# Adding the experts' rows into the token sums by the scatter itself (layer 1's MoE)

## What is computed

```
gate_logits = xf @ Wg + bg                      # xf = layernorm(t)
top_w, top_i = top_k(gate_logits, 2)
top_w = softmax(top_w)
w_dense = sum(one_hot(top_i, E) * top_w)
for e in range(E):
    h = gelu(xf @ W1[e] + b1[e])
    out = out + w_dense[:, e] * (h @ W2[e] + b2[e])
t = t + out                                     # then turned back to (channels, places)
```

## Time and profile before

| | us |
|---|---|
| median of 3 runs | 2480.7 (2469.35 to 2482.45) |
| the profiled execution, its own time | 2486.87 |
| its span in the trace | 2485.1 |

### The profile page before, as it was taken

How to read it: one execution, slowest core, us unless ns; L and a number is a source line. 1 busy time by engine, 2 the same in 40 slices (tenths; PEclk the granted TensorE clock), 3 DMA queues, 4 the chain that set the end, 5 groups by cost and what they waited for, 6 DMA issues and landing times. The chain is left out here.

```text
span 2485.1 us, 83832 instructions
## 1 busy us (share of the span) xinstructions
PE 2015.4 (81%) x28694; PEld 1524.5 (61%) x28695; DVE 2062.4 (83%) x3713; ACT 1732.2 (70%) x2708; POOL 790.9 (32%) x604
## 2 busy tenths in 40 slices
PE   6749999999999999999996208856896229999994
PEld 3327666666666766666664206643684129999992
DVE  5779999999999999999997646759797457777775
ACT  5569999999999999999984415537686335555551
POOL 3432124241431331231440553430364532222220
PEclk9869999999999999999997559985997559999996
DMA  2013323232323232323232233442112341111116
GB/s 81 1 34 89 84 77 89 72 92 70 92 71 91 71 90 71 90 72 89 73 85 84 87 131 104 116 126 95 45 68 84 112 135 51 48 47 47 51 44 209
DMA packets 285209, 202.98 MB, mean 82 GB/s; under 512 B 153395, under 2 KB 259846, under 8 KB 284870
## 3 DMA queue, kind: packets, MB, share of 16 engines
q1 hardware_dynamic: 271168, 163.57, 22.8%
q0 software_dynamic: 12960, 35.73, 3.9%
q10 hardware_dynamic: 998, 2.62, 0.3%
HBM read 68.98 MB, written 108.60 MB: 71 GB/s over the span
## 5 line engine op out<-in xcount | busy, mean ns | idle before, releaser
L595 DVE TENSOR_TENSOR plow<-prob 128x1024 f16<-128x1024 f32 (+1 forms) x1024 | 1127.1, 1171 | 3.7 <-ACT prob L506 3.7
L506 ACT ACTIVATE prob<-scores 128x1024 f32<-128x1024 f32 x1024 | 999.5, 1025 | 88.9 <-PE scores L638 58.5
L658 PEld LDWEIGHTS outp<-vs,prob 128*128 128x128 bf16 x7680 | 515.3, 98 | 279.8 <-issue 219.9
L658 PE MATMUL outp<-vs,prob 128*128 (+1 forms) x7680 | 603.6, 193 | 25.0 <-DVE plow L595 12.4
L638 PE MATMUL scores<-qT,kT 128*128 (+1 forms) x2048 | 610.6, 380 | 7.5 <-DMA kT<-shift_rows 2.7
L660 PE MATMUL outp<-vs,plow 128*128 (+1 forms) x7680 | 601.2, 193 | 0.0
L660 PEld LDWEIGHTS outp<-vs,plow 128*128 128x128 f16 x7680 | 502.8, 97 | 57.9
L448 POOL TENSOR_TENSOR osum<-osb 128x128 f32<-128x128 f32 x64 | 269.9, 4217 | 783.4 <-DVE rec L600 783.4
L1476 POOL DMA_INDIRECT expert_rows<-m1eyo,m1edest x71 | 108.0, 1521 | 304.5 <-DVE m1eyo L1448 275.5
L1347 PE MATMUL m1eph<-m1exT,m1ew1c 128*128 128x128 f16 x3408 | 203.4, 220 | 0.3 <-ACT m1exT L1384 0.3
L1347 PEld LDWEIGHTS m1eph<-m1exT,m1ew1c 128*128 128x128 f16 x3408 | 194.5, 98 | 1.0 <-ACT m1exT L1384 0.5
(11 more groups left out here) (393 smaller groups left out, 3335.4 us busy)
## 6 DMA issues: line engine op xcount, KB each, us to landing
sorted_rows<-zero SPq DMA_DIRECT2D x128, 522.0 KB, 4.7
staged<-qk SPq DMA_DIRECT2D x73, 128.0 KB, 2.3
m0exr<-sorted_rows SPq DMA_DIRECT2D x71, 130.5 KB
m1exr<-sorted_rows SPq DMA_DIRECT2D x71, 130.5 KB, 2.0
ls_got<-expert_rows SPq DMA_DIRECT2D x8, 1024.0 KB, 6.0
na_staged<-in_L_ffn_W_dram SPq DMA_DIRECT2D x16, 512.0 KB, 3.6
m1dstg<-in_L_ffn_W_dram SPq DMA_DIRECT2D x16, 512.0 KB
m1cgot<-expert_rows SPq DMA_DIRECT2D x8, 1024.0 KB
```

The costliest lines, as they stand in the source:

```text
L506: act.activation(prob[g % PBUF][:, :], scores[g % 2][:, :], ACT.Exp, scale=1.0 / (QK_SCALE * QK_SCALE)).then_inc(prob_ready, 1)
L595: dve.tensor_tensor(l[:, 0:n], p[:, 0:n], high(p)[:, 0:n], ALU.subtract).then_inc(low_ready, 1)
L658: pe.matmul(to, high(prob[g % PBUF])[:, cols], v, start=(g == 0 and i == 0 and j == 0), stop=False, skip_group_check=True)
```

## The change

`sums_dram` is a new tensor in DRAM, `token_sums`, of 8192 + 128 rows of 256 numbers.

- In the dispatch SP stores `tok` to it, by rows, in eight parts of 512 KB, one after each odd-numbered load of weights, and one tile more to its spare rows. It waits for all of them at its end.
- The tail of a row now holds the token's number (not twice it), the second expert's share and the difference of the two shares, both divided by 64. They are worked out in front of `slots`; the three operations after it are gone.
- In the experts, `b2t` lies in the space of `tok` and is scaled by 64 once. `aim` makes the row's share. ACT copies the result out of PSUM times that share (`share_rows`), and DVE adds share times `b2t`. POOL's scatter adds in DRAM and goes out only when the one before has landed.
- The last stage is `store_sums`: it fetches 4 MB in ten parts, all issued at once; PE turns pairs of tiles with 4 buffers, ACT and DVE copy them out in turn, SP stores them in nine parts. Nothing is added.

```diff
@@ dispatch, SP
                 sp.dma_start(wide(i), src).then_inc(w_in[i % 3], 16)
+                if sums_dram is not None and i % 2 and i // 2 < NT // 4:
+                    t = slice(i // 2 * 4, i // 2 * 4 + 4)
+                    sp.dma_start(sums_dram[0:S, :].rearrange("(t p) d -> p t d", p=P)[:, t, :], tok[:, t, :]
+                                 ).then_inc(sums_begun, 16)
+            if sums_dram is not None:
+                sp.dma_start(sums_dram[SPARE:SPARE + P, :], tok[:, 0, :]).then_inc(sums_begun, 16)
+                sp.wait_ge(sums_begun, 16 * (NT // 4 + 1))
@@ dispatch, DVE, route
+                if sums_dram is None:
+                    dve.tensor_copy(tails[:, s0:s0 + G, 1:1 + NR], ...
+                else:
+                    link(dve.tensor_scalar(tails[:, s0:s0 + G, 1:1 + NR],
+                                           tok2[:, t0:t0 + G].unsqueeze(2).broadcast_to([P, G, NR]), 1.0 / TOP, None,
+                                           ALU.mult))
...
+                if sums_dram is not None:
+                    dve.wait_ge(exped, g + 1)
+                    link(dve.tensor_scalar(w[0], r[:, :], 1.0, W_SCALE, ALU.add, ALU.mult))
+                    link(dve.reciprocal(w[0], w[0]))
+                    link(dve.tensor_tensor(tails[:, s0:s0 + G, 2], w[0], r[:, :], ALU.mult))
+                    link(dve.tensor_tensor(tails[:, s0:s0 + G, 3], w[0], tails[:, s0:s0 + G, 2], ALU.subtract))
                 dve.wait_ge(ranked, g + 1)
...
                 dve.tensor_copy(slots[g % 2][:, :, :], place[:, :, :]).then_inc(slots_ready, 1)
-                if not by_probs:
-                    dve.wait_ge(exped, g + 1)
-                    link(dve.tensor_scalar(w[0], r[:, :], 1.0, None, ALU.add))
-                    link(dve.reciprocal(w[0], w[0]))
-                    link(dve.tensor_tensor(w[1], w[0], r[:, :], ALU.mult))
@@ experts, PE, second
-                pe.wait_ge(y_taken, i + 1)
+                pe.wait_ge(y_shared if summed else y_taken, i + 1)
@@ experts, ACT
+            def share_rows(i, u):
+                act.wait_ge(y_ready, i + 3)
+                act.wait_ge(y_taken, i + 1)
+                act.activation(shared[u % 2][:, :], py[u % 2][:, 0:D], ACT.Copy, scale=share[u % U][:, 0:1]
+                               ).then_inc(y_shared, 1)
             def step(i, u, it, left):
                 if left > 1:
                     take_x(i + 2, u + 2)
                 if left > 0:
                     gelus(i + 1, u + 1)
+                if summed:
+                    share_rows(i, u)
@@ experts, DVE, aim
+                if summed:
+                    dve.scalar_tensor_tensor(out=is_first[u % 2][:, :], in0=tail[:, 0:1], scalar=tile_code[:, ds(i, 1)],
+                                             in1=tail[:, 3:4], op0=ALU.is_equal, op1=ALU.mult).then_inc(compared, 1)
+                    dve.tensor_copy(dest[u % U][:, :], tail[:, 1:2])
+                    dve.wait_ge(compared, i + 1)
+                    dve.tensor_tensor(share[u % U][:, :], is_first[u % 2][:, :], tail[:, 2:3], ALU.add).then_inc(aimed, 1)
+                    return
@@ experts, DVE, rows_out
+                if summed:
+                    dve.wait_ge(y_shared, i + 3)
+                    dve.scalar_tensor_tensor(out=yo[u % NY][:, :], in0=b2t[:, ds(e, 1), :].squeeze(1),
+                                             scalar=share[u % U][:, 0:1], in1=shared[u % 2][:, :], op0=ALU.mult,
+                                             op1=ALU.add).then_inc(y_taken, 1)
+                    return
@@ experts, DVE, start
             dve.wait_ge(b2_in, 16)
+            if summed:
+                dve.tensor_scalar(b2t[:, :, :], b2t[:, :, :], W_SCALE, None, ALU.mult).then_inc(b2_scaled, 1)
+                dve.wait_ge(b2_scaled, 1)
@@ experts, POOL
                 pool.wait_ge(y_taken, i + 3)
+                if summed and not (isinstance(i, int) and i == 0):
+                    last = (u - 1) % NY
+                    pool.wait_ge(y_out[last], uses(it, u - 1, NY) * 16 + 16)
                 pool.sem_inc(sending, 1)
                 to = bass.IndirectOffsetOnAxis(ap=dest[u % U][:, 0:1], axis=0)
-                pool.indirect_dma_start(out=y_dram, out_offset=to, in_=yo[u % NY][:, :], in_offset=None
-                                        ).then_inc(y_out[u % NY], 16)
+                pool.indirect_dma_start(out=y_dram, out_offset=to, in_=yo[u % NY][:, :], in_offset=None,
+                                        compute_op=ALU.add if summed else ALU.bypass).then_inc(y_out[u % NY], 16)
@@ store_sums in the place of combine_experts
+    CUTS = (0, 1, 2, 4, 8, 12, 16, 20, 24, 28, 32)
+        @block.sync
+        def _(sp):
+            for q in range(len(CUTS) - 1):
+                t = slice(CUTS[q], CUTS[q + 1])
+                sp.dma_start(got[:, t, :], src[:, t, :]).then_inc(arrived[q], 16)
+            ENDS = (2, 4, 6, 8, 10, 12, 14, 15, 16)
+            for n0, n1 in zip((0,) + ENDS, ENDS):
+                sp.wait_ge(taken[0], (n1 + 1) // 2)
+                sp.wait_ge(taken[1], n1 // 2)
+                c = slice(n0 * 2 * P, n1 * 2 * P)
+                sp.dma_start(dst[:, :, c], outc[:, :, c]).then_inc(stored, 16)
...
+                if n >= NB:
+                    pe.wait_ge(taken[n % 2], (n - NB) // 2 + 1)
+                for k in range(KB):
+                    for j in range(2):
+                        last = pe.transpose(pt[n % NB][:, k, j * P:(j + 1) * P], got[:, 2 * n + j, k * P:(k + 1) * P],
+                                            ident32[:, :])
...
+            for n in range(0, PAIRS, 2):
+                act.wait_ge(turned, n + 1)
+                act.activation(outc[:, :, pair(n)], pt[n % NB][:, :, :], ACT.Copy).then_inc(taken[0], 1)
...
+            for n in range(1, PAIRS, 2):
+                dve.wait_ge(turned, n + 1)
+                dve.tensor_copy(outc[:, :, pair(n)], pt[n % NB][:, :, :]).then_inc(taken[1], 1)
```

More of the change, by code:

```diff
@@ L935, in dispatch @@
         b_in = sem("b_in")
+        sums_begun = sem("sums_begun")
         b_turned = sem("b_turned")
@@ L1257, in experts @@
         w2h, w2l = w2[:, 0], w2[:, 1]
-        b2t = sb("b2t", [P, E_N, D], F32)
+        summed = room is not None
+        b2t = room[:, 0:E_N, :] if summed else sb("b2t", [P, E_N, D], F32)
         xr = [sb(f"xr{u}", [P, RW], F32) for u in range(NX)]
@@ L1492, in combine_experts @@
         outc = ctx.enter_context(nc.sbuf_tensor(name + "outc", [P, KB, S], F32))
-        pt = [ctx.enter_context(nc.psum_tensor(name + f"pt{u}", [P, KB, 256], F32)) for u in range(2)]
-        arrived = [semaphore(nc, name + f"arrived{b}") for b in range(NB)]
-        added = semaphore(nc, name + "added")
+        pt = [ctx.enter_context(nc.psum_tensor(f"{name}pt{u}", [P, KB, 2 * P], F32)) for u in range(NB)]
+        arrived = [semaphore(nc, f"{name}arrived{q}") for q in range(len(CUTS) - 1)]
@@ L1496, in combine_experts @@
         turned = semaphore(nc, name + "turned")
-        taken = semaphore(nc, name + "taken")
+        taken = [semaphore(nc, f"{name}taken{u}") for u in range(2)]
         stored = semaphore(nc, name + "stored")
         block = ctx.enter_context(nc.Block())
-        src = y_dram[0:TOP * S, :].rearrange("(t p c) d -> p t (c d)", p=P, c=TOP)
-        def fetch(eng, q):
-            if q >= NB:
-                eng.wait_ge(added, TOP * GC * (q - NB + 1))
-            eng.dma_start(got[q % NB][:, :, :], src[:, q * GC:(q + 1) * GC, :]).then_inc(arrived[q % NB], 16)
@@ L1507, in _ @@
-        @block.vector
-        def _(dve):
-            for t in range(NT):
-                if t % GC == 0:
-                    dve.wait_ge(arrived[t // GC % NB], 16 * (t // GC // NB + 1))
-                for c in range(TOP):
-                    if t or c:
-                        dve.wait_ge(added, TOP * t + c)
-                    dve.scalar_tensor_tensor(out=tok[:, t, :], in0=got[t // GC % NB][:, t % GC, c * D:(c + 1) * D],
-                                             scalar=weights[c][:, t:t + 1], in1=tok[:, t, :], op0=ALU.mult,
-                                             op1=ALU.add).then_inc(added, 1)
+        src = sums_dram[0:S, :].rearrange("(t p) d -> p t d", p=P)
@@ new lines, in store_sums @@
+        dst = out_dram.rearrange("b (k p) h w -> p (b k) (h w)", p=P)
+        part_of = lambda t: next(q for q in range(len(CUTS) - 1) if t < CUTS[q + 1])
+        pair = lambda n: slice(n * 2 * P, (n + 1) * 2 * P)
+        @block.sync
[9 more added lines that the diff above has]
+                sp.dma_start(dst[:, :, c], outc[:, :, c]).then_inc(stored, 16)
+            sp.wait_ge(stored, 16 * len(ENDS))
```

60 lines of the change are left out of this document (27 added, 33 removed).

## The result

The changed kernel took 2457.15 us (median of 8 runs, 2451.38 to 2469.99), the kernel before in the same runs 2478.69 (8 runs): ratio 0.9921, 95% interval 0.9905 to 0.9937. The forecast was 2470.9, as a ratio 0.9960. The time moved the way it was forecast and about twice as far, to 2.9 us under the lower end of the range. The profiled execution took 2460.1 us (span 2458.3).

A forecast was written before the change was run, and what follows sets the result against it. It took PE to bound the loop, DVE's routing and then DMA the dispatch, DVE's additions and DMA the last stage. Terms 2.4 + 4.0 + 1.5 + 0 + 2.3 - 20 = -9.8 us gave 2470.9, range 2460 to 2500.

The forecast's parts named there:

- Routing and stores: Layer 1's dispatch: operations added before `slots` cost +2.4 us, token stores among weight loads +4.0.
- the +2.9: Dispatch routing: +0.96 us on the path in each of groups 0, 1 and 2, before -0.5 in group 3.
- the stores' +4.0: Dispatch: token stores ahead of later weight loads in SP's ring delay them, +4.0 us, ends 0 and +8.
- The base: Whole kernel: the median before the change, 2480.7 us, from which the forecast subtracted 9.8.
- Start of the experts: Before the loop's first output: DVE scales the biases first, +1.5 us; +2.1 between the marks compared.
- The loop: Experts' loop: PE holds 5.52 us a tile, the added ACT, DVE and POOL work fits, cost 0.
- The cycle: Experts' loop: one serial adding scatter takes near 4.2 us (3.7 + 0.5), under the 5.52 us tile.
- End of the loop: Last two scatters, now serial, end later: +2.3 us, ends 0.6 and 4; +1.7 behind the last `yo`.
- Last stage: Final stage: half the fetch and all additions gone, DMA at 365 GB/s, 24.7 us instead of 44.6, -20.
- the dispatch that hides its additions: Rival in the dispatch: stores ride in what scatters leave, last stage runs at 389 GB/s; -16, 2465 us, chance 0.27.

The follow-up runs named there:

- longer_route_2: Kernel before with only the change's longer routing added in m1's dispatch, in lot D where semaphores come late: 2482.72 us, ratio 0.9975.
- calm lots: Timing lots B and E, where the kernel before took 2453.3 and 2454.9 us; the other lots are called late.
- longer_route: Kernel before with only the change's longer routing added in m1's dispatch, in lot B (kernel before 2453.3 us): 2457.69 us, ratio 1.0014.
- pair of spaced kernels: Kernel before and changed kernel, each with an awaited POOL memset between two tiles' scatters in both dispatches: 2470.14 and 2458.80 us in lot E.
- lot A: The runs of the main result, unedited changed kernel beside the kernel before: 2457.15 against 2478.69 us, ratio 0.9921.
- serial_plain: Changed kernel with scatters that overwrite instead of adding, each still waiting for the one before: 2458.54 us, ratio 0.9929.

## Why the prediction was wrong

- **Routing and stores, +6.4: the failing step.** It took the 8.24 and 8.37 us of idle POOL for the routing's own length, so that each operation added in front of `slots` had to show. In the profile of before most of that idle time was DVE waiting for late semaphores (6.67 us in front of group 2's routing). Where they come late, the added operations vanish behind them, and POOL's pauses got shorter (longer_route_2: -6.2 us). Where they don't, POOL has no such pause at all: in the seven profiles of calm lots it takes up each of m1's groups 1 to 3 0.30 us after the one before. The added operations then show once, at group 0 (+1.0), and not three times. longer_route's +3.4 agrees with the +2.9 in size, not in path. In the pair of spaced kernels, with the lateness out of both, m1's dispatch grew from 126.6 to 129.1 us: +2.5, for routing and stores together, of which 1.0 is group 0's routing and 1.3 in POOL's issuing of the four groups, 97.5 us instead of 96.2. So each operation was sized rightly, the path was wrong, and the stores' +4.0 was too much: hidden in calm lots and in the spaced pair. In lot A the dispatch got 3.9 us shorter and m0's, with the same code, 5.6.
- **The base.** The other half of the miss lies outside the change: the median from which I subtracted holds 24 to 25 us of lateness (2478.7 against 2454.9 and 2453.3), and the changed program's 12 to 14 (2457.2 against 2444.9 and 2443.0). That this is lateness and not another property of the lots rests on the spaced kernels, which differ between lots by 2.5 us (before) and 0.3 (changed). I had taken everything ahead of m1 as fixed; it moved by 8.5.
- **Start of the experts**, +2.1 with ACT's copy: +2.8 in A, +2.3 in the spaced pair (16.5 to 18.8). Right.
- **The loop**, 0: right, 384.2 and 384.1 us, no gap on PE. The cycle was mis-described: POOL's wait was ended by the scatter before it 47 times of 62, not by `yo`, and one adding scatter takes 4.0 to 5.4 us, where I had 3.7 + 0.5. So there was 0.1 to 1.5 us to spare, where I had counted on 1.3.
- **End of the loop**, +1.7 of it behind the last `yo`: +1.0 and +0.9. The second of the last scatters starts 4.66 us after the first (2419.66, 2424.32), 0.9 more than sized, but from there to the first fetch it is 7.6 us and no longer 8.6.
- **Last stage**, -20: -18.2, -17.9 in the spaced pair, -17.1 timed alone. DMA is the bound, as said, at 345 GB/s over the stage instead of 365; that is 1.3 of the 1.8 us.

Put together by the profiles of the spaced pair: +2.5 +2.3 -0.1 +0.9 -17.9 = -12.3 us, timed -11.3; forecast -9.8. The sum was nearly right for the change, and partly by luck, since 3.9 us too much for routing and stores stood against 2.1 too much gain from the last stage; it was wrong for the measurement. The rival that was nearest, the dispatch that hides its additions (-16, 2465), named the place but not the cause.

## To carry to other kernels

Before a wait is charged to an instruction, look when the work it waited for had ended; an idle time that starts after its releaser was done doesn't belong to the path that you price. Where nearly the same code runs twice in a profile, compare the two: m0's first groups started 24.6 and 25.2 us apart and m1's 28.7 and 28.8, though m0's routing has more operations (for group 0, which waits for nothing late, 8.3 us to `slots` and not 5.5). The length of the routing could not be what set the starts. A change that touches a stretch with such lateness should be timed with the lateness taken out on both sides too.

## What the runs showed of the hardware

- While POOL issues indirect scatters back to back (16 at a pitch of 1.28 us), semaphore increments of other engines can arrive late: in the profile of before PE's for DVE by 7.6 us (1959.36, 1966.97) and for ACT by 10. In all 29 late hand-offs at groups 1 and 2 DVE went on 2.1 to 2.9 us after the last of the sixteen scatters; spacing the issues took nearly all of it away. Some lots of runs show it and others don't, with the same chip number. Why was not found. The kernel before took 22 to 35 us more in the lots that show it, the changed one 12 to 21.
- A scatter of 128 KB that adds took 1.57 to 2.36 us to issue where one that overwrites took 1.35 (serial_plain; 1.51 in the kernel before), with 144 packets instead of 48 and 2.4 times the data time. From its start to POOL's next work it was 4.0 us in one program and 5.4 in another.
